# A tanh softplus, and the last stage's fill in another order, in a two-layer Perceiver kernel on one core

## The reference

```
u, z = silu(conv(x @ W_in[:256])), x @ W_in[256:]
dt_raw, B, C = split(u @ W_x)                     # 1, 16, 16 columns
dt = clip(softplus(dt_raw * W_dt + b_dt), 1e-4, 10.0)
A  = -exp(min(A_log, 5.0))
h  = clip(h * exp(clip(dt * A, -20, 0)) + clip(dt * B * u, -10, 10), -100, 100)   # 32 steps
y  = (layernorm(h . C) * g + b + D * u) * silu(z)
x  = x + y @ W_out
xa = layernorm(x) @ P_w                           # then: C1, C2, C3 = softmax over the top 3 of xa @ U
x  = x + sum_e C2[e] * W2[e] @ gelu(sum_e C1[e] * W1[e] @ x_normed) + C3 @ b2     # 12 experts
```

## Time and profile before

| | |
|---|---|
| median of 3 runs | 1869.2 us (1869.15 to 1873.27) |
| profiled execution | 1870.31 us, of which the span from the first to the last instruction is 1868.5 us |
| PE busy | 1580.0 us (85%) |
| VectorE busy | 1353.5 us (72%) |
| ScalarE busy | 1034.3 us (55%) |
| GpSimd busy | 521.2 us (28%) |
| granted TensorE clock, mean | 0.944 of full |

### The profile page before, as it was taken

One profiled execution on the slowest core, in us unless ns is written; L12 is line 12 of the kernel. 1 busy time (PEld: TensorE's weight loads), 2 busy tenths in 40 slices (PEclk: granted clock), 3 DMA queues, 4 the chain that ended last, 5 costly groups with the idle time before them and its releaser, 6 DMA issues. The chain is left out here.

```text
span 1868.5 us, 36875 instructions
## 1 busy us (share of the span) xinstructions
PE 1580.0 (85%) x10997; PEld 1031.1 (55%) x11024; DVE 1353.5 (72%) x3801; ACT 1034.3 (55%) x2779; POOL 521.2 (28%) x559
## 2 busy tenths in 40 slices
PE   5999999999998999799895885477777774999999
PEld 2666666666665455466563674366655563444444
DVE  4777777777777666577686444799999996677765
ACT  2666666666665333344332225899999992322321
POOL 1211111111111100000000721688888880322200
PEclk9999999999999999899897898798988886999999
DMA  5011011011010900000366000000000001000000
GB/s 136 24 34 34 23 34 34 23 34 34 23 34 5 349 8 0 1 1 1 97 212 183 0 0 0 1 1 0 0 0 0 0 0 51 1 7 6 12 6 17
DMA packets 69336, 66.48 MB, mean 36 GB/s; under 512 B 5695, under 2 KB 66834, under 8 KB 69266
## 3 DMA queue, kind: packets, MB, share of 16 engines
q1 hardware_dynamic: 66598, 64.00, 11.5%
q10 hardware_dynamic: 2668, 1.62, 0.3%
HBM read 61.41 MB, written 4.19 MB: 35 GB/s over the span
## 5 line engine op out<-in xcount | busy, mean ns | idle before, releaser
L1995 PE MATMUL ss_y_ps<-ss_h,ss_diag 128*128 128x256 f32 x1024 | 264.4, 422 | 133.8 <-ACT sc_dt L1913 93.2
L1995 PEld LDWEIGHTS ss_y_ps<-ss_h,ss_diag 128*128 128x128 f32 x1024 | 215.6, 214 | 182.4 <-issue 79.1
L595 ACT ACTIVATE x_probs<-x_probs,x_neg_max 128x257 f32<-128x257 f32 x512 | 253.5, 498 | 63.2 <-DVE x_neg_max L696 63.2
L696 DVE CUSTOM_DVE_ANT_0 x_probs<-x_s_ps,x_mask_b 128x257 f32<-128x257 f32 x512 | 187.3, 423 | 133.5 <-PE x_s_ps L403 133.5
L1897 ACT ACTIVATE ss_decay<-sc_dt,sc_a 128x256 f32 (+1 forms) x496 | 207.8, 479 | 1.8 <-DVE ss_h L1960 1.8
L1951 DVE SCALAR_TENSOR_TENSOR ss_decay<-ss_decay,ss_h 128x1024 f32<-128x1024 f32 x124 | 152.3, 1228 | 27.7 <-ACT ss_decay L1897 27.4
L1907 ACT ACTIVATE ss_come<-ss_dtu,sc_xd 128x256 f32<-128x256 f32 x384 | 163.6, 512 | 6.6 <-POOL ss_dtu L1853 6.6
L413 PE MATMUL x_pT_ps<-all_ident,x_probs 128*128 128x128 f32 x1024 | 162.4, 282 | 0.6 <-DVE x_pT L703 0.6
L1867 POOL TENSOR_TENSOR ss_diag<-all_ident,sc_xd 128x512 f32<-128x512 f32 x128 | 158.8, 1240 | 12.8 <-PE ss_y_ps L1995 2.9
L703 DVE COPY x_pT<-x_pT_ps 128x512 f32<-128x512 f32 x256 | 161.3, 668 | 0.5 <-PE x_pT_ps L413 0.5
L1960 DVE CUSTOM_DVE_ANT_0 ss_h<-ss_come,ss_decay 128x1024 f32<-128x1024 f32 x124 | 149.9, 1209 | 0.0
(11 more groups left out here) (373 smaller groups left out, 3072.0 us busy)
## 6 DMA issues: line engine op xcount, KB each, us to landing
x_ctx_t<-ctxT SPq DMA_DIRECT2D x48, 514.0 KB, 3.8
kept_ctx_t<-ctxT SPq DMA_DIRECT2D x16, 514.0 KB, 8.2
kept_ctx_n<-ctx SPq DMA_DIRECT2D x16, 512.0 KB, 8.5
x_ctx_n<-ctx SPq DMA_DIRECT2D x16, 512.0 KB, 4.1
all_x<-x SPq DMA_DIRECT2D x4, 512.0 KB, 7.8
x_mid<-all_x SPq DMA_DIRECT2D x32, 64.0 KB, 4.0
all_x<-x_mid SPq DMA_DIRECT2D x4, 512.0 KB, 7.6
out<-all_x SPq DMA_DIRECT2D x8, 256.0 KB, 2.0
```

Of the source, the lines that this page charges most:

```text
L595: ins = nc.scalar.activation(probs[p][:, n, :], probs[p][:, n, :], ACT.Exp, scale=-1.0, bias=neg_max[p][:, n:n + 1], accum_out=sums[p][:, ...
L696: vec.tensor_tensor_reduce(probs[p][:, n, :], s_ps[:, c, 0:S2], mask_b[:, :], -1.0, -MASKED, ALU.add, ALU.min, neg_max[p][:, n:n + 1]).the ...
L1995: ins = nc.tensor.matmul(y_ps[p][:, 0:DI], diag[q][:, m, :], h[q][:, m, :], start=(q == 0 and m == 0), stop=(q == NQ - 1 and m == NH - 1))
```

## The change

It has two parts. In the softplus, the term is taken as -ln(0.5 + 0.5 tanh(|v| / 2)). Tanh of each tile is taken inside the loop, one tile behind Abs; Ln follows behind the loop, then the Exp of `a`. The clip is now a clamp of the raw dt, tile by tile in the loop, at the values whose softplus is 1e-4 and 10. In the fill, PE's projection of group 1 is split in two halves with `turn_x(0)` between them; ScalarE's second `copy_vT` of group 1, `sqrt(1)` and `norm(1)` stand earlier; on VectorE, `centred` and `finish` of group 2 stand ahead of `add_projected(1)`, and `y_stats(3)` behind it.

```diff
+DT_LOW, DT_HIGH = float(np.log(np.expm1(1e-4))), float(np.log(np.expm1(10.0)))
 # scan_inputs, ScalarE
                     nc.scalar.activation(soft[:, t - 2, :], dt[:, t - 2, :], ACT.Abs).then_inc(abs_sb, 1)
+                if inside(t - 3):
+                    act.wait_ge(abs_sb, t - 2)
+                    act.sem_inc(waited, 1)
+                    nc.scalar.activation(soft[:, t - 3, :], soft[:, t - 3, :], ACT.Tanh, scale=0.5).then_inc(tanh_sb, 1)
...
-            pipeline(act, step, 2, 2, TAPS)
-            act.wait_ge(abs_sb, T)
+            pipeline(act, step, 2, 3, TAPS)
+            for q in range(LN_Q):
+                t = slice(q * LT, (q + 1) * LT)
+                act.wait_ge(tanh_sb, (q + 1) * LT)
+                nc.scalar.activation(soft[:, t, :], soft[:, t, :], ACT.Ln, scale=0.5, bias=half[:, :]).then_inc(ln_sb, 1)
             act.wait_ge(a_step, 1)
             nc.scalar.activation(a[:, :], a[:, :], ACT.Exp).then_inc(a_step, 1)
-            for half in range(2):
-                quarters = range(half * LN_Q // 2, (half + 1) * LN_Q // 2)
-                for q in quarters:
-                    s = slice(q * LT, (q + 1) * LT)
-                    nc.scalar.activation(soft[:, s, :], soft[:, s, :], ACT.Exp, scale=-1.0).then_inc(exp_sb, 1)
-                for q in quarters:
-                    s = slice(q * LT, (q + 1) * LT)
-                    act.wait_ge(exp_sb, q + 1)
-                    nc.scalar.activation(soft[:, s, :], soft[:, s, :], ACT.Ln, bias=1.0).then_inc(ln_sb, 1)
 # scan_inputs, VectorE
                     vec.scalar_tensor_tensor(dt[:, t - 1, :], w_dt[:, :], xd[:, t - 1, 0:1], b_dt[:, :],
-                                             ALU.mult, ALU.add).then_inc(dt_sb, 1)
+                                             ALU.mult, ALU.add).then_inc(raw_sb, 1)
+                    dve.wait_ge(raw_sb, t)
+                    vec.tensor_scalar(dt[:, t - 1, :], dt[:, t - 1, :], DT_LOW, DT_HIGH, ALU.max, ALU.min).then_inc(dt_sb, 1)
...
+            vec.memset(half[:, :], 0.5).then_inc(prep, 1)
...
-                vec.scalar_tensor_tensor(dt[:, s, :], dt[:, s, :], 0.0, soft[:, s, :], ALU.max, ALU.add).then_inc(soft_sb, 1)
-                dve.wait_ge(soft_sb, q + 1)
-                vec.tensor_scalar(dt[:, s, :], dt[:, s, :], 1e-4, 10.0, ALU.max, ALU.min).then_inc(clip_sb, 1)
+                vec.scalar_tensor_tensor(dt[:, s, :], dt[:, s, :], 0.0, soft[:, s, :], ALU.max, ALU.subtract).then_inc(soft_sb, 1)
 # stage_tail, PE
-            def project(m):
-                pe.wait_ge(vT_sb, 2 * m + 2)
-                wait(pe, mid_sb, m)
-                wait(pe, x_sb, m - 3)
-                for j in range(GT):
+            def project(m, halves=range(2)):
+                pe.wait_ge(vT_sb, 2 * m + halves[-1] + 1)
+                if halves[0] == 0:
+                    wait(pe, mid_sb, m)
+                    wait(pe, x_sb, m - 3)
+                for j in range(halves[0] * 2, halves[-1] * 2 + 2):
...
-            project(1)
+            project(1, (0,))
             turn_x(0)
+            project(1, (1,))
             address(0)
 # stage_tail, ScalarE
             copy_vT(1, 0)
+            copy_vT(1, 1)
             sqrt(0)
             norm(0)
-            copy_vT(1, 1)
             copy_xT(0)
             copy_address(0)
+            sqrt(1)
             copy_z(0)
-            sqrt(1)
+            norm(1)
             exps(0)
             copy_weights(0)
-            norm(1)
 # stage_tail, VectorE
             chain_e(0)
+            centred(2, range(GT))
+            finish(2, (0, 1))
+            finish(2, (2, 3))
+            add_projected(1)
             y_stats(3, range(GT))
-            add_projected(1)
             x_stats(1)
             chain_a(1)
             chain_b(1)
             chain_c(1)
-            centred(2, range(GT))
-            finish(2, (0, 1))
-            finish(2, (2, 3))
```

More of the change, by code:

```diff
@@ L1639, in scan_inputs @@
         soft = sb("soft", [P, T, DI])
+        half = sb("half", [P, 1])
         x_ps, c_ps, u_ps, d_ps = (ps(n, [P, BANK]) for n in ("x_ps", "c_ps", "u_ps", "d_ps"))
@@ L1648, in scan_inputs @@
         waited_pool = sem("waited_pool")
-        waited, abs_sb, exp_sb, ln_sb, soft_sb, clip_sb = (sem(n) for n in ("waited", "abs_sb", "exp_sb", "ln_sb", "soft_sb", "clip_sb"))
+        waited, abs_sb, tanh_sb, ln_sb, soft_sb, raw_sb = (sem(n) for n in ("waited", "abs_sb", "tanh_sb", "ln_sb", "soft_sb", "raw_sb"))
         block = ctx.enter_context(nc.Block())
@@ L1694, in step @@
                     ins.then_inc(xd_psum, 1)
-            pe.wait_ge(prep, TAPS + 2 + 9)
+            pe.wait_ge(prep, TAPS + 3 + 9)
             pipeline(pe, step, 2, 1, TAPS)
@@ L1795, in _ @@
             vec.tensor_scalar(a[:, :], a[:, :], 5.0, None, ALU.min).then_inc(a_step, 1)
-            dve.wait_ge(prep, 2)
-            split_row(vec, dve, prep, TAPS + 2, cb3[:, :], rowmask, (c_hi[:, :], c_rest[:, :], c_f[:, :]), cb[0:3, :])
+            dve.wait_ge(prep, 3)
+            split_row(vec, dve, prep, TAPS + 3, cb3[:, :], rowmask, (c_hi[:, :], c_rest[:, :], c_f[:, :]), cb[0:3, :])
             pipeline(dve, step, 3, 1, TAPS)
@@ L1801, in _ @@
                 dve.wait_ge(ln_sb, q + 1)
-                vec.scalar_tensor_tensor(dt[:, s, :], dt[:, s, :], 0.0, soft[:, s, :], ALU.max, ALU.add).then_inc(soft_sb, 1)
-                dve.wait_ge(soft_sb, q + 1)
-                vec.tensor_scalar(dt[:, s, :], dt[:, s, :], 1e-4, 10.0, ALU.max, ALU.min).then_inc(clip_sb, 1)
+                vec.scalar_tensor_tensor(dt[:, s, :], dt[:, s, :], 0.0, soft[:, s, :], ALU.max, ALU.subtract).then_inc(soft_sb, 1)
             dve.wait_ge(a_step, 2)
             vec.tensor_scalar(a[:, :], a[:, :], -1.0, None, ALU.mult).then_inc(a_step, 1)
-            dve.wait_ge(clip_sb, LN_Q)
+            dve.wait_ge(soft_sb, LN_Q)
 def scan_states(nc, g, uz, dt, xd, a):
@@ L2171, in project @@
                                  start=(c == 0), stop=(c == DB - 1))
-                ins.then_inc(q_psum, 1)
+                if halves[-1] == 1:
+                    ins.then_inc(q_psum, 1)
             def turn_x(n):
```

## The result

The changed kernel takes 1853.25 us (median of 4 runs, 1852.06 to 1854.5), the kernel before 1870.0 beside it (4 runs, 1869.15 to 1873.27): a ratio of 0.9905, 95% interval 0.9891 to 0.9919. Faster by 0.95% was measured; 1853.8 was predicted. The profiled execution took 1852.8 us, its span 1850.9, 17.6 less than before.

The account below looks back on a forecast made before the run. Bounds: PE and GpSimd in the loop, ScalarE's softplus behind it, a chain of short steps in the fill. Gains 11.9 + 0.2 + 3.3 = 15.4 from 1870.31 gave 1854.9, set to 1853.8 by the median; range 1850.7 to 1858.

Parts of the forecast that it names:

- Softplus, 11.9: Behind the scan's input loop: Exp, clip and table loads leave, VectorE sets the pace; gain 11.9 us, bounds 10.7 to 12.6.
- the drain's 0.67 for 0.66 of clamps: At the end of the scan's input loop: two of three clamps count, lengthening the drain by 0.66 us.
- Clamp and Tanh in the loop, 0: In the scan's input loop: idle time of VectorE and ScalarE hides the added clamp and Tanh; cost 0.
- The rival: In the loop: Tanh needs another table, two loads a tile; no change (2 in 100) or slower (2 in 100).
- Scan start, 0.2: At the first decays: a table load goes, but raw terms wait for GpSimd's third dtu; 0.2 us, bounds 0 and 1.28.
- Fill, 2.8 + 0.5: In the last stage's fill: earlier address matmul gains 2.8 us, PE's wait at group 1's turn goes, 0.5; together 3.3.
- the first term: In the fill: group 0's turn between projection halves starts the address matmul at 1568.1, not 1570.90; gain 2.8 us.
- the fast clock: PE's clock in the fill, a rival within the forecast's own range; 25 in 100.
- The low end, 1850.7: Lower end of the predicted time: the fast clock and the whole scan load, 1.1 us more.
- the scan load's 1.1: At the scan's start: the whole table load saved, 1.1 us more than forecast, counted in the low end.
- the root bounds z: In the fill, a rival: group 1's root exceeds its 0.35 us allowance, delaying z and lists; 1857.1 us; 12 in 100 for the fill's loss.
- The second term: In the fill: group 1's norm ahead of the Exp removes PE's 0.49 us wait at group 1's turn; gain 0.5 us.

Follow-up runs that it names:

- The two by two: Two runs on the changed kernel: group 1's projection whole, vT copy early, 1851.98 us; projection divided, copy behind the norm, 1851.14 us.

## Why the prediction was right, step by step

**Softplus, 11.9.** It held term by term: the drain's 0.67 for 0.66 of clamps, 0.60 for the 0.67 of two Tanh behind the last Abs (1149.66 to 1150.26), one load of 1.28, four Ln in 7.68 for 7.4, and VectorE as the pacemaker with 8.90 for 8.9, which covers the longer Ln. Measured 11.91 by S. That a's load and Exp are hidden held (done at 1160.79, the sign at 1162.43). **Clamp and Tanh in the loop, 0**: held, by the idle times above. The price of a clamp where GpSimd is full, 0.701 us, lay near the upper bound of 0.29 to 0.75, and the cover was enough for one, as the run with three shows from the other side.

**The tables.** The rival had 4 in 100 and did not come: no load stands in the loop. In the changed kernel the Tanh of 32 tiles stand among Silu, Copy and Abs without a load (one load, ahead of the first Silu, in 1030 to 1150), and in the run with Sigmoid each change between Sigmoid and Silu has one, of 1.28 us. Behind the loop Ln and a's Exp have one each, 1.28 us long (1150.28 and 1159.28), as the forecast had it.

**Scan start, 0.2.** From the change of sign to the second group of raw terms it was 14.05 us (1188.97 - 1174.92) and is 13.90 (1176.33 - 1162.43): 0.15, with the wait for GpSimd's dtu that was named in the place of the load.

**Fill, 2.8 + 0.5.** The mechanism and the sign were right, the first term was too small: 4.03 for 2.8. It took PE's lower level, a granted clock of 0.50 (3.79 us for a whole projection, 1.12 for a turn), for the halves and the turn. In the trace the first half took 1.06 and the turn 0.66, at a granted clock of 1.00, for 1.9 and 1.1; the second half took 1.35, at 0.73, and only the address and ranking were as before (1.97, 1.92, at 0.50). From the start of the turn to that of the address matmul it is 1.78 us (1554.14 - 1552.36) where the forecast had 1.1 + 1.9: this is the difference of 1.2. The forecast gave the fast clock 25 in 100, and it came in part: the rows of turn and second half are 0.44 and 0.55 shorter. But address and ranking ran at 0.50, so the root was in time (1558.05, z at 1558.80) and did not bound z. The low end, 1850.7, lies 3.1 under the forecast; beside the scan load's 1.1 that leaves 2.0 for the fast clock, and no run shows this term. What the runs show is L in this order of the fill: 25.24 with halves and turn at 0.50 (address at 0.71, ranking at 1.00), 24.61 in the changed kernel, and 23.67 with halves, turn, address and ranking all at 1.00. That the root bounds z was seen where address and ranking were fast too: with the projection whole the ranking is done at 1557.49, and z, at 1558.59, stands behind the root at 1558.47. The run with three clamps shows the case that was forecast, with PE at the lower level:
```profile
1556.66 1.12 PE L2184 MATMUL tl_m_ps<-all_ident,tl_xn 128*128 128x128 f32 x4 [1.19 <-ACT tl_xn L2304]
1557.57 1.91 PE L2176 MATMUL tl_o_ps<-sc_w_o,tl_vT 128*128 128x128 f32 x8
1559.41 1.48 PE L2189 MATMUL tl_m_ps<-tl_xnT,sc_w_a 128*64 128x512 f32 x2
```
There the address matmul starts 20.80 us behind the stage's first load (1559.41 - 1538.61), before 23.55 (1570.90 - 1547.35): 2.75 for the 2.8 forecast. So the path held, and what the forecast had wrong was the level of the clock.

One reason in that step was wrong. It saw the gain in the turn no longer standing behind the projection. The two by two shows that the division was not needed: with the copy of vT ahead of the norm, the whole projection ends before the norm does. What cost time before took both, a late copy and a turn behind the whole projection: together they put the projection in front of a turn whose input was ready.

The second term, PE's wait at group 1's turn, was 0.69 for 0.5. Behind it came 0.35 that no step named: from the first list to that turn it was 11.97 before (1587.96 - 1575.99) and is 11.62 with that wait put back. VectorE's twelve MAX8 stood in two rows with a pause of 0.23 between them then, 1.55 in all, and take 1.21 now. This is not the fill's doing: the run with the fill alone has the pause too, and the runs with the softplus alone and with the clip alone, which have the fill before, go without it (11.61 and 11.60 from the first list to that turn). The cause stays open.

**Sum.** 11.91 + 0.15 + 4.03 + 0.69 + 0.35 = 17.1 by the trace, 15.4 forecast; the medians differ by 16.75. The rest of the span's 17.6 is about the loop's earlier start (0.58), ahead of the change. That the time itself came within 0.55 us of 1853.8 is partly luck: the gain was 1.35 larger than forecast, and the kernel before took 0.8 more beside it than the 1869.2 from which the forecast was counted.

## What to carry to other kernels

Take a function into a loop that waits elsewhere when no load comes with it (here Tanh beside Silu had none, Sigmoid beside Silu two of 1.28 us a tile, and S was 128.90 and 160.90), and count the idle time that is left at the fullest stretch before taking it. In the run with Sigmoid the load for Silu stood behind Silu's wait for PE, and the idle time ahead of it hid nothing (14.6 us ahead of 27 loads): look on which side of a load the idle time stands. When two edits aim at one wait, undo each alone: here either was enough, and the plainer one (the copy's place) left a better order open.

## What the runs showed of the hardware

The same order of the fill gave L of 23.67 (with the fill alone, and with Sigmoid), 24.61 and 25.24; the rows that differ are PE's, by the level of its clock: eight ranking matmuls took 1.08 us at a granted clock of 1.00 and 1.92 at 0.50, and four of the turn 0.66 at 1.00 or 1.12 at 0.50. The idle time just ahead does not by itself tell which level a step gets: the turn ran at 1.00 after 2.71 us without work in the changed kernel, and at 0.50 after 1.19 us in the run with three clamps, behind a half of 1.92 us at 0.50. And the price of a VectorE instruction was not one number: the clamp of 256 columns took 0.701 us on average in 1048 to 1081, where GpSimd was busy 30.46 of 33 us, and 0.294 in 1085 to 1145, where it was busy 10.23 of 60; with three clamps, where VectorE had no idle time left before its copies, the first of them took 0.581 in 1048 to 1081.
